# Sums added by the transfers themselves, and more tiles of the last stretch split into two halves

## The reference, cut to what matters

```python
h = relu(layernorm(x))
mask = (adj < 0.5) & ~eye
sens = exp(-(1 / r - 1 / mu) ** 2 / (2 * sigma ** 2))      # r = adj where mask, else 1
x = x + where(mask, sens, 0) @ (h @ W0 + B0)                # layer 1
h = relu(layernorm(x))
x = x + (adj * adj + eye) @ (h @ W1.T)                      # layer 2
```

## Time and profile before

| | us |
|---|---|
| median of 3 runs | 1907.28 |
| lowest and highest | 1904.74, 1908.49 |
| the profiled execution, its own time | 1907.14 |
| its span, first to last instruction | 1905.3 |
| busy in the span: PE / DVE / ACT / POOL | 1850.5 / 1732.5 / 1733.1 / 111.6 |
| mean granted clock of TensorE, share of full | 0.991 |

### The profile page before, as it was taken

One profiled execution on the slowest core, in us unless ns is written; L12 is line 12 of the kernel. 1 busy time (PEld: TensorE's weight loads), 2 busy tenths in 40 slices (PEclk: granted clock), 3 DMA queues, 4 the chain that ended last, 5 costly groups with the idle time before them and its releaser, 6 DMA issues.

```text
span 1905.3 us, 13395 instructions
## 1 busy us (share of the span) xinstructions
PE 1850.5 (97%) x4820; PEld 886.4 (47%) x4820; DVE 1732.5 (91%) x1024; ACT 1733.1 (91%) x986; POOL 111.6 (6%) x201
## 2 busy tenths in 40 slices
PE   6989999999999999999999999999999999999997
PEld 4544443444444444444444444444444445555554
DVE  7999999998999999999999999999999955678776
ACT  7999999898999999999999999999999988777552
POOL 0000001100000000000000000000000000000112
PEclk9999999999999999999999999999999999999999
DMA  7576887797868687767776686666566577667995
GB/s 264 204 287 255 317 306 278 302 342 284 346 240 337 252 320 283 279 253 276 269 272 241 264 307 238 255 242 231 227 231 226 198 277 279 270 247 302 338 372 229
DMA packets 84289, 521.19 MB, mean 274 GB/s; under 512 B 11008, under 2 KB 11392, under 8 KB 28032
## 3 DMA queue, kind: packets, MB, share of 16 engines
q1 hardware_dynamic: 68544, 468.94, 64.6%
q0 software_dynamic: 15680, 51.39, 7.4%
HBM read 492.50 MB, written 27.79 MB: 273 GB/s over the span
## 4 chain that ended last, share of the span: by engine, by line
PE 31%; DVE 24%; ACT 23%; issue 18%; DMA 3%; POOL 1%; DVEq 0%; POOLq 0%; SPq 0%
PE p_x L483 9%; PE p_l1a L449 9%; DVE rings L624 8%; DVE rings L617 8%; ACT rings L792 7%; ACT rings L797 7%; ACT rings L802 6%; PE p_l1b L449 6%; DVE rings L635 5%; PE p_own L483 4%; ACT rings L810 2%; DMA acc_dram<-xa_buf 1%; DMA outT<-xa_buf 1%; DMA x_buf<-xT 1%; DVE xa_buf L734 1%
## 5 line engine op out<-in xcount | busy, mean ns | idle before, releaser
L624 DVE SCALAR_TENSOR_TENSOR rings<-rings,small 128x2048 f32<-128x2048 f32 x256 | 599.8, 2343 | 24.3 <-ACT rings L797 24.1
L617 DVE SCALAR_TENSOR_TENSOR rings<-rings 128x2048 f32<-128x2048 f32 x256 | 584.4, 2283 | 8.3 <-PE p_l1b L449 7.7
L802 ACT ACTIVATE rings<-rings,small 128x2048 f32<-128x2048 f32 x256 | 533.2, 2083 | 46.2 <-DVE rings L624 45.8
L792 ACT ACTIVATE rings<-rings,small 128x2048 f32<-128x2048 f32 x256 | 509.5, 1990 | 13.7 <-DVE rings L617 9.7
L483 PE MATMUL p_x<-rings,h 128*128 128x512 f32 x1128 | 512.6, 599 | 8.7 <-DVE xa_buf L729 4.8
L797 ACT ACTIVATE rings<-rings 128x2048 f32<-128x2048 f32 x256 | 488.0, 1906 | 5.5
L449 PE MATMUL p_l1b<-rings,h 128*128 128x512 f32 x1024 | 459.7, 595 | 0.0
L449 PE MATMUL p_l1a<-rings,h 128*128 128x512 f32 x1024 | 457.5, 593 | 0.7 <-DVE h L681 0.7
L483 PEld LDWEIGHTS p_x<-rings,h 128*128 128x128 f32 x1128 | 215.5, 192 | 274.7 <-issue 263.2
L635 DVE TENSOR_TENSOR rings<-rings 128x2048 f32<-128x2048 f32 x135 | 308.3, 2284 | 6.6 <-DMA rings<-adjT 3.3
L449 PEld LDWEIGHTS p_l1b<-rings,h 128*128 128x128 f32 x1024 | 195.3, 191 | 243.7 <-issue 241.6
(11 more groups left out here) (95 smaller groups left out, 575.1 us busy)
## 6 DMA issues: line engine op xcount, KB each, us to landing
rings<-adjT SPq DMA_DIRECT2D x439, 1024.0 KB, 6.9
xa_buf<-acc_dram POOLq DMA_DIRECT2D x77, 256.0 KB, 6.5
acc_dram<-xa_buf POOLq DMA_DIRECT2D x74, 256.0 KB, 5.8
x_buf<-xT SPq DMA_DIRECT2D x32, 256.0 KB, 5.4
outT<-xa_buf POOLq DMA_DIRECT2D x16, 256.0 KB, 7.8
acc_dram<-y_buf POOLq DMA_DIRECT2D x15, 256.0 KB, 5.4
y_buf<-acc_dram POOLq DMA_DIRECT2D x13, 256.0 KB, 4.6
acc_dram<-x_buf POOLq DMA_DIRECT2D x1, 256.0 KB, 5.2
```

The costliest lines, as they stand in the source:

```text
L617: dve.scalar_tensor_tensor(out=tile(s_ring, slot_of(t)), in0=tile(a_ring, slot), scalar=CUTOFF, in1=tile(a_ring, slot), op0=ALU.is_lt, op1 ...
L624: dve.scalar_tensor_tensor(out=v, in0=v, scalar=neg_2c, in1=v, op0=ALU.add, op1=ALU.mult).then_inc(squared, 1)
L792: act.activation(v, v, ACT.Ln, bias=tiny_c).then_inc(ln_done, 1)
L802: act.activation(v, v, ACT.Exp, bias=exp_bias, scale=neg_k).then_inc(sens_done, 1)
```

## The change: what it does, and the diff

1. All 64 items that can be split are split. By their number r among the splits, those with r % 5 in (1, 3), 26 of 64 (12 of the last 29), have their high half copied by ScalarE right behind its square; the other 38 by VectorE as before. VectorE writes all low halves. Each waits for the high half of whichever engine wrote it.
2. `acc_dram` is gone. Every sum goes to `outT` by a DMA that adds to what stands there (`accum_op=ALU.add`); the first one of a row writes plainly. GpSimd waits ahead of each for the transfer of the same row before it. No sum is loaded back: the 77 loads into `xa_buf` and 13 into `y_buf` are gone, with the 13 adds of line 712. All 90 chains leave PSUM by the plain copy.

```diff
-SPLITS = [it for it in ITEMS if it.step >= LAST + SPLIT_STEP.get(it.source, STEPS) and it.row != it.source
-          and it.m % 5 % 2 == 0]
+SPLITS = [it for it in ITEMS if it.step >= LAST + SPLIT_STEP.get(it.source, STEPS) and it.row != it.source]
 for r, it in enumerate(SPLITS):
     it.split = r
+    it.high_by = "act" if r % 5 in (1, 3) else "dve"
+    it.highs = len([x for x in SPLITS[:r + 1] if x.high_by == it.high_by])
...
                 dve.wait_ge(q_by[it.by], it.squares)
-                if it.split < 3:
-                    dve.wait_ge(s_used, LAST)
-                else:
-                    dve.wait_ge(q_used, SPLITS[it.split - 3].m + 1)
-                dve.tensor_copy(high[:, :], squares).then_inc(high_ready, 1)
-                dve.wait_ge(high_ready, it.split + 1)
+                if it.high_by == "dve":
+                    if it.split < 3:
+                        dve.wait_ge(s_used, LAST)
+                    else:
+                        dve.wait_ge(q_used, SPLITS[it.split - 3].m + 1)
+                    dve.tensor_copy(high[:, :], squares).then_inc(high_by["dve"], 1)
+                dve.wait_ge(high_by[it.high_by], it.highs)
                 dve.tensor_tensor(low_ring[it.load % A_RING][:, :], squares, high[:, :].bitcast(F32),
                                   ALU.subtract).then_inc(low_ready, 1)
...
             def add_y(c):
                 dve.wait_ge(x1_added, c + 1)
-                if c in PRIORS:
-                    dve.wait_ge(prior_loaded, 16 * (PRIORS.index(c) + 1))
-                    dve.tensor_tensor(y_buf[:, :], y_buf[:, :], x_buf[c % 2][:, :],
-                                      ALU.add).then_inc(prior_added, 1)
-                    dve.wait_ge(prior_added, PRIORS.index(c) + 1)
-                elif c >= 2:
+                if c >= 2:
                     dve.wait_ge(y_stored, 16 * c)
                 dve.wait_ge(q_used, OWN_LAST[c] + 1)
-                dve.tensor_tensor(y_buf[:, :], p_own[c % 2][:, :],
-                                  (y_buf if c in PRIORS else x_buf[c % 2])[:, :],
+                dve.tensor_tensor(y_buf[:, :], p_own[c % 2][:, :], x_buf[c % 2][:, :],
                                   ALU.add).then_inc(y_ready, 1)
...
                 dve.wait_ge(q_used, ch.last_m + 1)
-                if state_before(ch) is None:
-                    if k >= XA_RING:
-                        dve.wait_ge(xa_stored[k % XA_RING], 16 * (k // XA_RING))
-                    dve.tensor_copy(buf[:, :], p_chain[ch.bank][:, :]).then_inc(xa_added, 1)
-                else:
-                    loads = len([o for o in CHAINS[:k + 1]
-                                 if o.index % XA_RING == k % XA_RING and state_before(o) is not None])
-                    dve.wait_ge(xa_loaded[k % XA_RING], 16 * loads)
-                    dve.tensor_tensor(buf[:, :], p_chain[ch.bank][:, :], buf[:, :], ALU.add).then_inc(xa_added, 1)
+                if k >= XA_RING:
+                    dve.wait_ge(xa_stored[k % XA_RING], 16 * (k // XA_RING))
+                dve.tensor_copy(buf[:, :], p_chain[ch.bank][:, :]).then_inc(xa_added, 1)
...
                 act.activation(a, a, ACT.Square).then_inc(q_by["act"], 1)
+                if it.split is not None and it.high_by == "act":
+                    act.wait_ge(q_by["act"], it.squares)
+                    if it.split < 3:
+                        act.wait_ge(s_used, LAST)
+                    else:
+                        act.wait_ge(q_used, SPLITS[it.split - 3].m + 1)
+                    act.activation(high_ring[it.split % 3][:, :], a, ACT.Copy).then_inc(high_by["act"], 1)
...
             def store_chain(ch):
                 pool.wait_ge(xa_added, ch.index + 1)
-                pool.dma_start(columns(outT if ch.final else acc_dram, ch.row),
-                             xa_buf[ch.index % XA_RING][:, :]).then_inc(xa_stored[ch.index % XA_RING], 16)
+                how = wait_before(ch.row, ch)
+                pool.dma_start(columns(outT, ch.row), xa_buf[ch.index % XA_RING][:, :],
+                               accum_op=how).then_inc(xa_stored[ch.index % XA_RING], 16)
```

More of the change, by code:

```diff
@@ L192 @@
     ch.before = [x for x in CHAINS[:ch.index] if x.row == ch.row]
-EVENTS = sorted([(ch.end + 2, 1, ch.row, ch) for ch in CHAINS if not ch.final]
+EVENTS = sorted([(ch.end + 2 + (S_STEPS if ch.final else 0), 1, ch.row, ch) for ch in CHAINS]
                 + [(NC * (c + 1) + 5, 0, c, None) for c in range(NC)], key=lambda e: e[:3])
[L197 to L220, removed]
+BEFORE, LATEST = {}, {}
+for _, _, row, ch in EVENTS:
+    BEFORE[(row, ch)] = LATEST.get(row)
+    LATEST[row] = (row, ch)
 EVAC_AFTER, TRANSFERS = {}, []
@@ L229 @@
     TRANSFERS.append((ch.store, 0, ch.index))
[L230 to L236, removed]
     ch.after = [o for o in CHAINS[:ch.index] if o.bank == ch.bank]
@@ L246 @@
     TRANSFERS.append((first_item(NC * (c + 1) + 5) + 0.1, 2, c))
-    if c in PRIORS:
-        TRANSFERS.append((first_item(NC * c + 13), 3, c))
 TRANSFERS.sort()
@@ L261, in sem @@
             return ctx.enter_context(nc.semaphore(name))
-        acc_dram = nc.dram_tensor("acc_dram", [D, N], F32).ap()
         h1 = sb("h1", [P, NC * G, D])
@@ L328, in gnn_program @@
         q_used = sem("q_used")
-        high_ready = sem("high_ready")
+        high_by = {"dve": sem("high_by_dve"), "act": sem("high_by_act")}
         low_ready = sem("low_ready")
@@ L351, in gnn_program @@
         h2_ready = sem("h2_ready")
-        prior_added = sem("prior_added")
         y_ready = sem("y_ready")
         y_stored = sem("y_stored")
-        prior_loaded = sem("prior_loaded")
-        xa_loaded = [sem(f"xa_loaded{n}") for n in range(XA_RING)]
         xa_added = sem("xa_added")
@@ L878, in _, with wait_before @@
                                pattern=[[-1, P]], channel_multiplier=1).then_inc(eye_ready, 1)
+            def wait_before(row, ch):
+                if BEFORE[(row, ch)] is None:
+                    return ALU.bypass
+                _, other = BEFORE[(row, ch)]
+                if other is None:
+                    pool.wait_ge(y_stored, 16 * (row + 1))
+                else:
+                    pool.wait_ge(xa_stored[other.index % XA_RING], 16 * (other.index // XA_RING + 1))
+                return ALU.add
             def store_y(c):
@@ L884, in store_y @@
                     pool.wait_ge(y_ready, c)
[L885 to L893, removed]
-                    pool.wait_ge(xa_stored[ch.index % XA_RING], 16 * (ch.index // XA_RING + 1))
-            def load_prior(c):
-                if c > 1:
-                    pool.wait_ge(y_stored, 16 * c)
-                wait_state(prior_of(c))
-                pool.dma_start(y_buf[:, :], columns(acc_dram, c)).then_inc(prior_loaded, 16)
-            def load_state(ch):
-                if state_before(ch) is None:
-                    return
-                k = ch.index
-                if k >= XA_RING:
-                    pool.wait_ge(xa_stored[k % XA_RING], 16 * (k // XA_RING))
-                wait_state(state_before(ch))
-                pool.dma_start(xa_buf[k % XA_RING][:, :], columns(acc_dram, ch.row)).then_inc(
-                    xa_loaded[k % XA_RING], 16)
+                how = wait_before(c, None)
+                pool.dma_start(columns(outT, c), (x_buf[0] if c == 0 else y_buf)[:, :],
+                               accum_op=how).then_inc(y_stored, 16)
             def store_chain(ch):
                 pool.wait_ge(xa_added, ch.index + 1)
-                pool.dma_start(columns(outT if ch.final else acc_dram, ch.row),
-                             xa_buf[ch.index % XA_RING][:, :]).then_inc(xa_stored[ch.index % XA_RING], 16)
+                how = wait_before(ch.row, ch)
+                pool.dma_start(columns(outT, ch.row), xa_buf[ch.index % XA_RING][:, :],
+                               accum_op=how).then_inc(xa_stored[ch.index % XA_RING], 16)
             for _, kind, n in TRANSFERS:
@@ L919, in _ @@
                     store_chain(CHAINS[n])
-                elif kind == 1:
-                    load_state(CHAINS[n])
-                elif kind == 2:
+                else:
                     store_y(n)
-                else:
-                    load_prior(n)
 def kernel(x, adj, L0_gnn_W, L0_gnn_B, L0_gnn_mu, L0_gnn_sigma, L1_gnn_W):
```

1 line of the change is left out of this document (removed).

## The result

The changed kernel takes 1925.16 us (median, 1922.99 to 1926.77), the kernel before in the same series 1904.24 (1902.09 to 1908.49). The ratio is 1.0105, 95% interval 1.0095 to 1.0115: 1% slower. The profiled execution took 1924.67 us with a span of 1922.7, against 1907.14 and 1905.3; the two profiles are thus 17.5 us apart and the medians 20.9, since the profiled run of before lay 3 us above its median. What follows compares the profiles.

What follows compares the result with a forecast made beforehand. TensorE was taken to set the pace of the last 350 us, VectorE to become the tail's bound. Span 1905.3 + 14.6 (VectorE) - 2 (rows) + 1 (last transfer) = 1918.9, with 1.8 outside 1920.7: forecast 1921 us, range 1907 to 1930.

Steps and rivals of the forecast that it cites:

- A: Stretch from the start to adding the x of row 14; 1563.6 us in the kernel before.
- B: Stretch from the x of row 14 to that of row 15, walked step by step; end forecast at 1796.5 us.
- Unit prices: Times per operation from the trace: split item saves TensorE 0.69 us; VectorE low half 2.21, high half 1.26; ScalarE copy 1.85.
- Up to step 249: VectorE still follows TensorE there; step 250 begins on VectorE 4.1 us earlier, at 1672.9.
- Rows 3 to 14: Thirteen VectorE adds removed, 9.2 us, counting only where TensorE waits: 0 to 9 us gained, 2 taken.
- The tail: From adding the x of row 15 to item 254's low half: VectorE work 103.8 us, with waits 107.4, until 1903.9.
- The end: After item 254's low half: 16.0 us kept, plus 1 for the last adding transfer (0 to +6.5).
- ScalarE's copies, which wait for split r - 3: ScalarE's added high halves: price 0; otherwise 1.85 us for each of nine in the dense steps, 17 at most.
- (a): Rival: VectorE avoids the dense steps' waits for ScalarE's squares, 9.2 us less: 1911.5 us, 1908 to 1914; chance 0.16.
- (b): Rival: TensorE stays the bound to the end as VectorE works ahead; 18.6 us gained, 1889 us; chance 0.04.
- (d): Rival: adding transfers are slow in the tail, 14 us more, 1935 us, or ScalarE's r - 3 waits bind; chance 0.12.
- (c): Rival: VectorE's relief in rows 3 to 14 counts in full, 7 us more, together with (a): 1904 us; chance 0.05.

Runs made afterwards that it cites:

- e12: Kernel before with only the new adding transfers, plus a spare VectorE add in each of 13 rows where line 712 stood: 1905.2 us, ratio 1.0003.
- e2: Kernel before with only the new splits and ScalarE's copies, sums still loaded back: 1931.98 us, ratio 1.0137.
- e6: Changed kernel with four spare TensorE matmuls in each of two gaps, ahead of items 221 and 252: 1922.18 us, ratio 1.0094.
- e3: Changed kernel with every transfer writing plainly instead of adding, same waits: 1925.58 us, ratio 1.0101.
- e5: Changed kernel with low halves written for 128 of 2048 columns, TensorE reading the high half instead (result rounded): 1890.61 us, one run.
- e9: As e5, with high halves up to step 255 all on VectorE, the tail's still two in five on ScalarE: 1879.98 us, one run.
- e4: Changed kernel with all 64 high halves on VectorE: 1943.9 us, one run.

## Why the prediction was right, and where its terms were off

The direction, the range and the reason held: slower, because VectorE becomes the bound. The forecast of 1921 lay 4 us below the median. It was built on a profiled run of before that lay 3 us above that kernel's median, so the change itself was forecast at 14 us and measured at 20.9 between medians. By its own steps, in profiles: forecast +13.6 us of span, measured +17.4. That it came as near as this is in part luck: A came 4.2 us earlier than forecast and B took 6.2 longer, and the two errors hide each other.

- **Unit prices.** All held. ScalarE's copy takes 1.92 us by itself with a pace of 1.82 (1.85 taken); an evacuation without its add 0.60.
- **Up to step 249.** Right. Without what the rows before gave, step 250 begins at 1666.6 + 6.2 = 1672.8; forecast 1672.9.
- **Rows 3 to 14: wrong, 2 us taken and 5.3 measured** (from row 2, -0.9, to row 14, -6.2). The failed step is that the 9.2 us would "count only where TensorE waits". TensorE at 1171 of 1180 us looked like the bound. But VectorE is at 1146 in the same row, and from 545 to 646 us at 100.4 of 101.2. TensorE's busy time didn't show what the adds cost: from the x of row 3 to that of row 12 it takes 902.8 us before and 897.6 after, with the same number of matmul records; TensorE's gaps shrink by 1.5 us and its busy time by 3.6, at a granted clock of 0.99 and 1.00. By the marks each of rows 4 to 7 gained 0.6 to 0.7 us, nearly one removed add per row, and e12 shows that it was the adds. The two adds between the x of rows 12 and 14 gained nothing (217.2 us in both kernels, 218.6 in e12). The -0.9 ahead of row 3 isn't of the change: e2, with the old transfers, has 0.5 of it, and in other traces it varies by as much.
- **Stretch B: forecast 232.9 us (1563.6 to 1796.5), measured 239.1.** The walk step by step was right in its shape (steps 251 to 256: 18.2, 15.3, 19.9, 17.2, 18.4, 8.0 us measured, 18.2, 15.3, 19.0, 17.0, 18.3, 8.0 forecast). Step 250 took 17.6 for 15.1: VectorE waited 3.1 us for a square and 0.8 for a copy of ScalarE there, where the walk had 1.5. ScalarE had stood still 5.9 us for the `premask` of the step before, and its squares and the copy came late by that; this is read from the timeline, no run tests it. From the start of step 257 to the x of row 15 it took 15.3 for 12.7: 2.4 us of it are the lower clock on TensorE, on the path to that x; e6 gives them back.
- **The tail: forecast 107.4, measured 108.1.** VectorE stands still only for the two small steps, 2.29 and 1.93 us (2.3 and 1.3 forecast), and no buffer of a sum ever makes it wait there.
- **The end: forecast 17.0, measured 18.1.** The adding transfer costs some 0.3 us, not 1: from the last evacuation's start to the end 9.7 us, for 9.4 before (9.6 to 9.8 in the other runs with adds that were compared, 9.4 in e2; e3, which writes plainly, took 10.5, so a single trace says little). But item 252 ran at the lower clock, 4.2 us for 2.74, and what is behind it waited; e6 gives back 1.3.
- **ScalarE's copies, which wait for split r - 3: priced at 0.** VectorE waits for copies 1.9 us in all from step 250 to the x of row 15 and never in the tail, though ScalarE itself waits 17.6 us for buffers ahead of them from 1677 us on.

The clock had been named as what would make the time later and had no term in the sum. It is worth 3.7 us of span in all (2.4 and 1.3 by e6). That this is also the size of the whole miss is a coincidence, as the errors in A and B show. Of the rivals, (a) fell: the waits for ScalarE's squares and copies from step 250 to the x of row 15 are 13.8 us, more than the 9.2 of the walk, and e5 and e9 show a reason, as ScalarE is a bound of its own in the dense steps. (b) and (d) fell (e4, e3). (c) was half right: the relief in the rows counts, 5.3 of the 9.2 us, but it didn't make the kernel faster. Of the signs, line 592 (624 before) of step 251 came 6.3 us earlier (2.5 forecast) and that of step 256 5.5 later (8 forecast): both some 3 us ahead, by what the rows had gained.

That the whole difference of the two kernels is in marks A to D, and that these move with VectorE's work (e4, e5, e12) and TensorE's clock (e6), is shown. Not tried: the fallen clock in steps 252 to 254, where VectorE is busy 19.9 of 20 us from 1700 us on and TensorE doesn't seem to be on the path, and other orders of ScalarE's program.

## What to carry to other kernels

Work that is moved from the bound to an engine with "20% to spare" has to be summed in the stretch where it is done, and item by item: 3.27 us on VectorE against 2.74 on TensorE settled the tail of this case. The slack in the earlier steps was not saved up, and VectorE's waits from 1540 to 1677 us say where it went:

```profile
DVE xa_buf L691 <- PE p_x L451: 29.2, 3, 17.8
DVE high L621 <- ACT rings L767: 6.9, 6, 1.9
DVE xa_buf L691 <- PE p_x L431: 5.7, 2, 3.6
```

VectorE runs in program order and stood 34.9 us ahead of evacuations whose chain TensorE hadn't finished; by the trace it never waited for TensorE to release one of the three high buffers. Whether evacuations placed later would have let it work ahead wasn't tried, nor were more buffers.

When two engines feed each other tile by tile, both at 97% or more, a microsecond taken off either one can count nearly in full (5.4 of 6.2 us here): put it back as spare work to see whose it was. Once an engine that was never idle gets gaps, look at its granted clock before pricing what is behind a gap.

## What the runs showed of the hardware that I had not expected

- TensorE's granted clock fell to its lower level within single gaps. After 4.4 us without a matmul, all 12 matmuls of item 221 ran at 1.2 GHz, for 5.2 us; after 3.4, the first 7 of item 252, with starts 0.43 us apart, and the rest 0.23. The average over a stretch hid it: 0.95 from 1677 to 1780 us, 0.71 from 1780 to 1790.
- A queue of 106 transfers, 90 of which add, takes 2.35 times the DMA engines' time of the same bytes written plainly (8.7 and 3.7%), in 14240 packets for 8480, and GpSimd 0.82 us to issue one for 0.59:

```profile
L867 POOL DMA_DIRECT2D outT<-xa_buf x90 | 73.8, 820 | 1460.2 <-DVE xa_buf L691 1397.3
```

```profile
L867 POOL DMA_DIRECT2D outT<-xa_buf x90 | 52.8, 586 | 1481.0 <-DVE xa_buf L691 1481.0
```

The first is of the changed kernel, the second of e3. Issue to landing took 6.7 us in the median with the adds and 4.8 without. VectorE and TensorE never waited for one; GpSimd waited once, 6.6 us, for a row's transfer before.
